# Setup of a post-norm layer kernel reordered: sign matrices transposed by DMA, the third chunk projected before the first feed-forward product

## The reference

```
r = sigmoid(x @ Wr.T);  k = x @ Wk.T;  v = x @ Wv.T
scale[t] = sigmoid(decay) ** t
state = cumsum(k * v / max(scale, 1e-10), axis=time) * scale
y = rmsnorm(r * state) * ln_w
x = layernorm(x + y @ Wo.T)
bw1 = mean|w1| per row * sign(w1);  bw2 = mean|w2| per row * sign(w2)
h = gelu(x @ bw1.T + b1)
out = layernorm(x + h @ bw2.T + b2)
```

## Time and profile before

| | us |
|---|---|
| median of 3 runs (851.1 to 851.57) | 851.55 |
| the profiled execution | 851.19 |
| its span | 849.6 |
| TensorE busy | 817.2 (96%) |
| VectorE busy | 754.1 (89%) |
| ScalarE busy | 685.4 (81%) |
| GpSimd busy | 336.1 (40%) |

### The profile page before, as it was taken

The page is one execution under the profiler, slowest core; times in us unless marked ns, Lnnn a source line. Parts: engine busy times, 40 slices in busy tenths (PEclk is TensorE's granted clock), DMA queues, the critical chain, the costliest instruction groups (busy, mean ns, idle before and its releaser), DMA issues.

```text
span 849.6 us, 16935 instructions
## 1 busy us (share of the span) xinstructions
PE 817.2 (96%) x5393; PEld 532.7 (63%) x5393; DVE 754.1 (89%) x1400; ACT 685.4 (81%) x976; POOL 336.1 (40%) x571
## 2 busy tenths in 40 slices
PE   6889999999999999999999999999999999999974
PEld 4556666666666666666666666666666666666653
DVE  3978999999999999999999999999999999999865
ACT  5798888888888888888888888888888888888745
POOL 4423334443333444333344433344433334443323
PEclk9999999999999999999999999999999999999988
DMA  8104443445534344553434455343445534334322
GB/s 227 46 25 100 94 98 92 110 105 123 123 87 110 77 111 108 123 123 80 110 82 109 113 123 123 76 109 88 105 117 123 117 80 101 97 77 97 75 52 73
DMA packets 165669, 85.23 MB, mean 100 GB/s; under 512 B 125968, under 2 KB 161296, under 8 KB 165648
## 3 DMA queue, kind: packets, MB, share of 16 engines
q1 hardware_dynamic: 142560, 51.39, 25.9%
q0 software_dynamic: 4608, 16.78, 10.2%
q10 hardware_dynamic: 18480, 16.79, 6.3%
HBM read 20.45 MB, written 16.78 MB: 44 GB/s over the span
## 4 chain that ended last, share of the span: by engine, by line
PE 89%; ACT 4%; DVE 3%; DMA 2%; issue 1%; POOL 1%; SPq 0%; ACTq 0%; POOLq 0%; DVEq 0%
PE ps_r L342 27%; PE ps_o L458 24%; PE ps_f L413 19%; PE ps_r L413 6%; PE ps_o L369 6%; PE ps_o L374 3%; PE ps_s L349 2%; DMA proj_in<-in_L_attn_Wr_dram 1%; ACT hid_hi L683 1%; ACT hid L646 1%; DMA x_t<-x_st 1%; POOL clip_g L1302 0%; ACT clip_g L711 0%; PE ps_o L471 0%; PE ps_r L471 0%
## 5 line engine op out<-in xcount | busy, mean ns | idle before, releaser
L458 PE MATMUL ps_o<-w2T,hid_hi 128*128 128x256 f16 x992 | 219.9, 274 | 0.5 <-DVE hid_lo L955 0.5
L458 PE MATMUL ps_o<-w2T,hid_lo 128*128 128x256 f16 x992 | 219.9, 274 | 0.0
L342 PE MATMUL ps_r<-x_t,proj_hi 128*128 128x512 f16 x768 | 198.6, 382 | 2.8 <-DVE k_sb L867 1.4
L646 ACT ACTIVATE hid<-ps_f,b1c,f_scale 128x512 f32<-128x512 f32 x192 | 145.3, 773 | 56.3 <-PE ps_f L413 51.1
L413 PE MATMUL ps_f<-x_t,w1T 128*128 128x512 f16 x768 | 181.9, 379 | 0.7 <-DMA x_t<-x_st 0.7
L1216 POOL TENSOR_TENSOR y_sqs<-y_sq 128x512 f32<-128x512 f32 x32 | 46.7, 1459 | 307.0 <-ACT y_sq L621 307.0
L955 DVE SCALAR_TENSOR_TENSOR hid_lo<-hid,hid_scale,hid_hi 128x1024 f16<-128x1024 f32 (+1 forms) x136 | 159.8, 1216 | 5.9 <-ACT hid_hi L683 5.3
L342 PEld LDWEIGHTS ps_r<-x_t,proj_hi 128*128 128x128 f16 x768 | 74.9, 98 | 94.0 <-issue 4.0
L683 ACT ACTIVATE hid_hi<-hid,hid_scale 128x2048 f16<-128x2048 f32 (+1 forms) x72 | 128.8, 1790 | 3.8 <-ACT hid L646 1.4
L413 PEld LDWEIGHTS ps_f<-x_t,w1T 128*128 128x128 f16 x768 | 75.0, 98 | 78.4 <-issue 0.9
L342 PE MATMUL ps_r<-x_t,proj_lo 128*128 128x512 f16 x384 | 114.3, 380 | 0.0
(11 more groups left out here) (171 smaller groups left out, 1419.0 us busy)
## 6 DMA issues: line engine op xcount, KB each, us to landing
x_in<-in_L_attn_x_dram SPq DMA_DIRECT2D x32, 512.0 KB, 3.8
res<-b_row POOLq DMA_DIRECT2D x32, 512.0 KB, 4.6
out_dram<-res ACTq DMA_DIRECT2D x31, 512.0 KB, 3.1
w_in<-in_L_ffn_w_dram SPq DMA_DIRECT2D x2, 1024.0 KB, 15.4
x_t<-x_st SPq DMA_TRANSPOSE x59, 4.3
b_row<-in_L_ffn_b_dram ACTq DMA_DIRECT2D x1, 512.0 KB, 12.3
out_dram<-res SPq DMA_DIRECT2D x2, 256.0 KB, 2.1
proj_in<-in_L_attn_Wk_dram SPq DMA_DIRECT2D x1, 256.0 KB, 5.2
```

Of the source, the lines that this page charges most:

```text
L342: last = nc.tensor.matmul(ps_r[:, m, :], w[:, m, dc, ec * P:(ec + 1) * P], xx[:, :, dc, :], start=(n == 0), stop=(n == 3 * DC - 1))
L458: last = nc.tensor.matmul(o_tok[:, tt, :], hh[:, hc, tt * P:(tt + 1) * P], w2T[:, hc, :], start=(hc == 0 and n == 0), stop=(hc == HC - 1 a ...
L646: nc.scalar.activation(hid[:, hc, :], f1_bank[hc % NF], ACT.Gelu, bias=b1c[:, hc:hc + 1], scale=f1_scale[:, hc:hc + 1]).then_inc(s_gelu, 1)
```

## The change

- w1 and w2's signs are transposed by two DMA transposes of SP, straight into w1T and w2T. The 32 transposes, their four copies and ident16 go. The layouts of w1T and w2T change: F2's moving operand is now two pieces of 128 columns, 2 KB apart, where it was one of 256.
- b1 and b2 are loaded by SP, after x chunk 2, and no more by ScalarE's queue.
- Wr's maximum, scale and split come after the splits of Wk and Wv; the idle transposes are 4 and no longer 12; `sum_wmax` for Wr stands behind R(0)'s first group.
- x chunk 2 is transposed into ps_f (the third slot), so R(2) runs whole ahead of T1(0), O(1) and F1(0).
- y of chunk 1 has its own buffer, the space of x1_st (`y_second`).
- All four quarters of clip_g are cut to 1 on GpSimd. `alphas1` and `alphas2` write over w1_in and w2_in.
- The high parts of hidden tiles 2, 3, 6 and 7 of chunk 0 are made on GpSimd; norm1(1) is done on VectorE.
- The loop's body has the same order of work on every engine. Its start is moved along the list on VectorE, ScalarE and GpSimd, so that some of the first step's work stands in the prologue.

The diff, cut to its core:

```diff
@@ sync
             load(2, 0, 2)
+            sp.dma_start(b1c[:, :], b1.rearrange("(c p) -> p c", p=P),
+                         allow_slow_non_contiguous=True).then_inc(s_b1_in, 16)
+            sp.dma_start(b2_row[:, :, :], b2.rearrange("(o n d) -> o n d", o=1, n=1).to_broadcast(
+                [P, TT, D])).then_inc(s_b2_in, 16)
             load(3, 0, 3)
+            sp.wait_ge(s_sgn, 1)
+            sp.dma_start(w1T[:, :, :, :].rearrange("p hc dc t -> p (hc dc) t"),
+                         w1_sgn[:, :, :].rearrange("p hc d -> p (hc d)"), transpose=True).then_inc(s_w1T, 16)
+            sp.wait_ge(s_sgn2, 1)
+            sp.dma_start(w2T[:, :, :, :].rearrange("p dc hc t -> p (dc hc) t"),
+                         w2_sgn[:, :, :].rearrange("p dc h -> p (dc h)"), transpose=True).then_inc(s_w2T, 16)
@@ tensor, F2
-                                                        w2T[:, hc, :], start=(hc == 0 and n == 0),
+                                                        w2T[:, :, hc, :], start=(hc == 0 and n == 0),
@@ tensor, prologue
-                pe.wait_ge(s_ident, 2)
+                pe.wait_ge(s_ident, 1)
                 TX(0, 0, 0, True)
                 sum_xbound(0)
                 for n in range(3):
                     proj_transposes(n)
...
-                for n in range(3 * TT):
+                for n in range(TT):
                     nc.tensor.transpose(ps_f[:, 1, 0:P], ident[:, :], ident[:, :])
-                R(0, True, looped=False, ecs=(0,), ms=range(2))
+                R(0, True, looped=False, ecs=(0,), ms=(0,))
+                pe.wait_ge(s_wscl, 2)
+                sum_wmax(ps_wmax[:, 2:3], 2, 1, 3)
+                R(0, True, looped=False, ecs=(0,), ms=(1,))
                 pe.wait_ge(s_wscl, 3)
                 sum_xbound(1)
                 R(0, True, looped=False, ecs=(0,), ms=(2,))
-                pe.wait_ge(s_setup_ev, 3)
                 wo_transposes()
                 sum_wmax(ps_womax, 3, 2, 5)
                 TX(1, 0, 1, True, slot=1)
                 R(0, True, looped=False, ecs=(1,))
-                R(1, False, looped=False, ecs=(0,), slot=1)
-                pe.wait_ge(s_xtmp, 2)
-                sum_bounds(0, 0)
-                w1_transposes()
+                R(1, False, looped=False, ecs=(0,), slot=1, ms=range(2))
+                sum_bounds(0, NCH)
+                R(1, False, looped=False, ecs=(0,), slot=1, ms=(2,))
+                pe.wait_ge(s_setup_v, 2)
+                TX(2, 0, 2, True, slot=2)
                 R(1, False, looped=False, ecs=(1,), slot=1)
                 O(0, 0)
+                R(2, False, looped=False, ecs=(0,), slot=2, ms=range(2))
                 pe.wait_ge(s_ms, 1)
-                sum_xbound(2)
-                TX(2, 0, 2)
-                pe.wait_ge(s_xtmp, 3)
-                sum_bounds(1, 0)
-                w2_transposes()
-                R(2, False, looped=False, ecs=(0,), ms=range(2))
-                pe.wait_ge(s_wcopy, 2)
+                sum_bounds(1, NCH)
+                R(2, False, looped=False, ecs=(0,), slot=2, ms=(2,))
+                R(2, False, looped=False, ecs=(1,), slot=2)
                 T1(0, 0, True)
+                sum_wmax(ps_wmax[:, 5:6], 5, 1, 6)
                 O(1, 1)
-                pe.wait_ge(s_ms, 2)
-                sum_wmax(ps_wmax[:, 5:6], 5, 1, 6)
-                F1(0, NCH, range(NF))
-                pe.wait_ge(s_ready, 2)
-                sum_xbound(3)
-                F1(0, NCH, range(NF, HC))
+                pe.wait_ge(s_w1T, 16)
+                F1(0, NCH, gates=3)
                 pe.wait_ge(s_xtmp, 4)
                 alpha2_to_row()
-                pe.wait_ge(s_gelu, 6)
-                R(2, False, looped=False, ecs=(0,), ms=(2,))
-                R(2, False, looped=False, ecs=(1,))
+                pe.wait_ge(s_w2T, 16)
@@ vector, setup
+            for n in range(2):
+                proj_maximum(n)
+                proj_scale(n)
+            xl(0, 0)
+            proj_split_lo(0)
+            proj_split_lo(1)
+            proj_maximum(2)
+            proj_scale(2)
+            dve.wait_ge(s_wscl, 3)
+            nc.vector.tensor_scalar_mul(w_inv[:, 2:3], w_inv[:, 2:3], 0.5).then_inc(s_winv, 1)
+            proj_split_lo(2)
@@ vector, prologue (all of it after the change)
                 wo_maxima()
                 take_xbound(1, 1)
                 dve.wait_ge(s_clip, 1)
                 kvs(0, 0, 0)
                 scans(0, 0, 0)
                 wo_scale()
                 dve.wait_ge(s_clip, 2)
                 kvs(0, 0, 1)
                 xl(1, 1, slot=1)
                 wo_split_lo()
                 scans(0, 0, 1)
                 take_bounds(0, 2)
                 dve.wait_ge(s_clip, 2 * DC)
                 kvs(1, 1, 0)
                 scans(1, 1, 0, y_second)
                 yl(0)
                 xl(2, 2, slot=2)
                 kvs(1, 1, 1)
                 mean_sq(0)
                 scans(1, 1, 1, y_second)
                 residual1(0, 0, first=True)
                 ustats(0)
                 dve.wait_ge(s_clip, 3 * DC)
                 kvs(2, 2, 0)
                 take_bounds(1, 3)
                 norm1(0, 0, 0)
                 yl(1, y_second)
                 hidden_bound()
                 x1l(0)
                 mean_sq(1)
                 scans(2, 2, 0)
                 hidden_scale()
                 residual1(1, 1)
                 ustats(1)
                 diagonal()
                 hl(0, pairs[0], first=True)
                 norm1(1, 0, 1)
                 hl(0, pairs[1], first=True)
                 hl(0, pairs[2], first=True)
                 x1l_rows(1, 1)
                 hl(0, pairs[3], first=True)
                 kvs(2, 2, 1)
                 scans(2, 2, 1)
                 dve.wait_ge(s_row, TT // 2)
@@ scalar, prologue (all of it after the change)
                 proj_split_hi(0)
                 proj_split_hi(1)
...
                 clip_table(0)
                 proj_split_hi(2)
                 xsq(1, 0, 1)
                 r_gates(0, 0, (0,))
                 xh(1, 1, slot=1)
                 wo_split_hi()
                 clip_table(1)
                 r_gates(0, 0, (1,))
                 ysq(0, (0,))
                 xsq(2, 0, 2)
                 ysq(0, (1,))
                 r_gates(1, 1, (0,))
                 yh(0)
                 xh(2, 2, slot=2)
                 signs(w1_in, w1_sgn, s_w1_in, s_sgn)
                 clip_table(2)
                 r_gates(1, 1, (1,))
                 signs(w2_in, w2_sgn, s_w2_in, s_sgn2)
                 act.wait_ge(s_ysqs, 1)
                 ysq(1, y=y_second)
                 xsq(3, 0, 3, looped=True)
                 alphas1()
                 r_gates(2, 2, (0,))
                 yh(1, y_second)
                 alphas2()
                 x1h(0, 1)
                 clip_table(3)
                 r_gates(2, 2, (1,))
...
                 gelu(0, range(0, 2))
                 act.wait_ge(s_ready, 2)
                 hh(0, pairs[0])
                 gelu(0, range(2, 4))
                 gelu(0, range(4, 6))
                 hh(0, pairs[2])
                 gelu(0, range(6, 8))
                 x1h_rows(1, 1)
                 xh_rows(3, 3)
                 take_alpha2_row()
@@ gpsimd, prologue (from the second chunk's clip on)
                 clip_min(1)
                 y_scale(0)
                 y_unscale(0)
+                scales(2, 2)
                 ysqs(0)
+                unscales(2, 2)
                 root_rms(0)
-                scales(2, 2)
-                unscales(2, 2)
+                clip_min(2)
                 root_u(0)
                 y_scale(1)
                 y_unscale(1)
                 ysqs(1)
+                scales(3, 3)
                 root_rms(1)
-                scales(3, 3)
                 unscales(3, 3)
+                clip_min(3)
+                pool.wait_ge(s_ready, 2)
+                root_u(1, True)
+                hh_odd(0, pairs[1])
+                hh_odd(0, pairs[3])
+                pool.wait_ge(s_b2_in, 16)
```

243 lines of the change are left out of this document (110 added, 133 removed).

## The result

The changed kernel takes 849.65 us in the median of 18 executions (847.39 to 851.69), the kernel before 851.56 on the same chip. The ratio is 0.9977, 95% interval 0.9968 to 0.9987: 1.9 us gained, where 6.3 were forecast. The profiled execution took 850.96 (span 849.2).

A forecast was written before the change was run, and what follows sets the result against it. TensorE (89%) bounds the kernel, with time to win only ahead of R(3): 3.1 + 6.4 - 3.8 + 0.8 = 6.5, less 0.2 for hand-overs, 6.3 us, so 845.2 us; forecast's own range 843.8 to 846.6, for all 842.3 to 848.8.

The forecast's parts named there:

- Step 1: The front: Wr lands near 9 us, not 12.05; R(0) starts at 12.45, not 15.82, first group at half pace.
- Steps 2 and 3: First k at 18.3 against 20.52; VectorE in series to the second y at 28.6; O(0) ends at 38.9 against 39.65.
- Step 4: R(2) whole, its fourth group at 44.4 after k(2); F1(0) at 52.9 against 55.97, F2(0) can start at 60.3 against 69.75.
- Step 5: F2(0) waits for operands, 3.8 us of new waits, last pair at 66.7; F1(1) starts at 71.1 against 77.56.
- Rival (b): GpSimd is the new bound; a clip or hh_odd 1 us longer at both places moves F1(1) by 2: 847.2; chance 0.13.
- Without waits it takes 64 x 0.109 = 7.0: F2(0) in step 5: its matmuls at full pace take 7.0 us, so ending at 71.1 means 3.8 us of new waits.
- every microsecond won there should reach the end: Setup ahead of R(3) at 87.83 us: time won there passes whole to the end, as steps stay at 24.86 us.
- Rival (d): w2T's new layout slows F2's matmuls: gain gone at 3.2 ns a matmul, 855 us at 5 ns; chance 0.03.
- (a): Front: Wr comes no earlier, being bound by latency; R(0) starts at 14.0, 1.6 us later than forecast: 846.8; chance 0.13.
- (c): Waits in step 5 are less; only F2(0)'s 7.0 us stand after 60.3, F1(1) at 69: 843; chance 0.11.
- (e): Reordering gives nothing: a gate holds F1(0) until 56 and F2(0) waits 3 us more for its pairs: 851.5; chance 0.05.
- the 5.3 us for b2's 512 packets: Loads of b1's small pieces and b2 ahead of x chunk 3: hidden, but would cost 5.3 us with their cover gone.

The follow-up runs named there:

- the one other with 67.3: Kernel before with both sign matrices transposed by SP's DMA and 14 + 9 idle matmuls in TensorE's wait at 41 to 46.7 us: 851.66 us, ratio 0.9996.
- the three edits: Changed kernel with quarter 3's clip on VectorE, chunk 0's last hid_hi on ScalarE, the unrolled step's first hid_lo pair behind kvg: 845.63 us, ratio 0.9925 to before.

## Why the prediction was wrong

The sign was right, and so was the new order's effect up to F2(0); the size was not. None of the 28 executions of the changed kernel came down to 845.2 (the lowest took 846.98).

- **Step 1** held, and its price for the first group was too careful: full pace (1.02) and not half, in return R(0) 0.55 later, since proj_lo ended at 12.9. The share of rows 4 was read rightly: Wr landed at 8.4.
- **Steps 2 and 3** held: first k at 17.58 (18.3), second y at 27.7 (28.6), both a little early.
- **Step 4** held in kind: the fourth group waited for k(2) as forecast, 44.68 (44.4); F1(0) 53.45 (52.9), F2(0) could start at 61.18 (60.3). The 0.2 taken off for hand-overs did not cover these 0.3 to 0.9, but they didn't delay R(3): VectorE reached residual1(1) at 54.58 (54.5), and TensorE waited for its pairs in F2(0) anyway.
- **Step 5 failed**, in the sentences "Then norm1(1), 2.3, to 61.9" and "The second pair comes at 63.1, the third at 64.3". The last pair came 1.9 late: 1.05 for norm1, and 0.9 for the two hid_lo ops beside hid_hi. Of the 1.05, GpSimd's clip of quarter 3 (the change's own move: two ops of 1.9 us for one of 0.7 on VectorE) gave back 0.3 when it was removed; the rest stayed, since u_rstd then collided with the first hid_lo (1.93 us for 1.03). The step also contradicts itself: it lets norm1(1) start at 59.6, while its own time for GpSimd, 61.8 for root_u and one hh_odd of 1.38, has root_u end near 60.4, and norm1 needs its result. I had taken each engine's durations as if the other were still. Rival (b) named the engine and the size (2 us); it was given 0.13.
- **"Without waits it takes 64 x 0.109 = 7.0"** failed next. I added 3.8 us of new waits to F2(0) and kept full pace behind them. Rows of before showed the counterexample: the earlier trace rows has TensorE idle for 3.81 us and the 16 transposes behind it took 1.82, against 1.05 for the 16 at 31.02. The cost here was 2.5 us in the profiled execution and near 0 in the next two. The forecast had no term for it.
- **"every microsecond won there should reach the end"** failed. The loop passed the gain on exactly (695.95 us from R(3) to R(31) in both kernels), the unrolled step did not: a pause of 0.53 us on VectorE and a u_ve 0.32 us later behind it turned a lead of 0.27 us into a lag of 0.17, and that cost 1.2 us. The runs without the collision have 65.2 to 66.2 us at the end, those with it 67.0 to 67.8 (the one other with 67.3 had the late transpose).
- **Rival (d)** fell: F2's matmuls have a mean of 277 ns against 274, and 273 in the kernel with the three edits. With the step unchanged at 24.86 us, w2T's new layout shows no cost; the 3 ns go with the clock. (a), (c) and (e) fell as well.
- **A price that does not follow**: the 5.3 us for b2's 512 packets. At 0.20 us a packet they are 512 x 0.20 / 16 = 6.4. Nothing in the forecast rests on it.

In sum, of the 4.4 us that the median of 18 stands above the forecast: 1.9 the late last pair, of which the three edits took back 1.3 to 1.4 (R(3) 83.05 and 83.25 against 81.75) and the collision that they left holds most of the rest; 1.2 the collision at the end; and what remains, 1.3, goes with the clock, which cost about 2.5 in F2(0) of the profiled execution. The last share is what is left over, not a measurement. With the three edits the median is 845.63. That this is 0.4 from the forecast is in part luck: it still has one collision, and its profile had no low clock in F2(0).

## What to carry to other kernels

Where a stage's sum goes by durations from a stage in which the other engine was still, look for the pairs that will now run side by side: a GpSimd op that reads SBUF and a VectorE op with two SBUF inputs take turns, and 0.1 us of lead decides whether a GpSimd op of 1.2 us takes 1.2 or 4.4. Moving one of a pair away can bring the next pair together, so look at the durations again after each edit. A wait that replaces work on TensorE isn't worth the work's time: add what the matmuls behind it may cost at 0.50 of the clock, as a range, since it differs between executions of the same program. And a gain in the setup has to be followed through the unrolled steps at the end, not only through the loop.

## What was not expected

- The same program came out of its low stretch of the clock at 68.6, 69.0 or 73.5 us, and its R(3) lay up to 2.4 us apart. A comparison of two kernels by one profile each can't tell less than that here.
- Two edits meant for the setup (hh_odd first, hid_hi on ScalarE) gained most at the far end, where they changed when GpSimd takes up u_ve.
- VectorE pauses for 0.53 us ahead of u_mv at one place of the unrolled step, and the pause goes when VectorE has one instruction more ahead of the loop. In the kernel before there is one of 0.16 between two u_mv.
- A DMA transpose of x1 took 5.9 to 6.6 us once or twice in each of four executions, where 4.3 is the median.
